# Centring, spread and norm products moved inside the two row scans

## The reference, cut to what matters

```python
def _L2_conv_ref(x, W):                 # layer 4's is the same with its own W
    rows = jnp.moveaxis(x, 1, 0)
    def step(carry, row):
        new = row + jax.nn.relu(conv1d_same(carry, W))     # 9 taps along the row
        return (new, new)
    _, outs = jax.lax.scan(step, rows[0], rows[1:])
...
def _ln_t(v, eps=1e-05):                # over the channels
    m = jnp.mean(v, axis=-1, keepdims=True); s = jnp.var(v, axis=-1, keepdims=True)
    return (v - m) / jnp.sqrt(s + eps)
...
x = x + _L2_conv_ref(_ln_c(x), L2_conv_W)          # scan 0
t = t + _L2_ffn_ref(_ln_t(t), ...)                 # experts, begins with gate logits of the norm
x = x + _L3_conv_ref(_ln_c(x), L3_conv_W)          # scan 1
t = t + _L3_ffn_ref(_ln_t(t), ...)                 # RNN: Wx, its mean and variance over the batch, 256 steps
```

## Time and profile before

| | |
|---|---|
| median of 3 runs | 385.49 us (384.47 to 387.49) |
| profiled execution, its own time | 385.72 us |
| its span (first to last instruction) | 383.9 us |
| mean granted clock of TensorE | 0.983 |
| PE busy | 346.4 us (90%) |
| DVE busy | 229.1 us (60%) |
| ACT busy | 191.1 us (50%) |
| chain that ended last, by engine | PE 64%, DVE 15%, ACT 13% |
| of it, row matmuls of the two scans (line 1076) | 6% |

### The profile page before, as it was taken

The page is one execution under the profiler, slowest core; times in us unless marked ns, Lnnn a source line. Parts: engine busy times, 40 slices in busy tenths (PEclk is TensorE's granted clock), DMA queues, the critical chain, the costliest instruction groups (busy, mean ns, idle before and its releaser), DMA issues.

```text
span 383.9 us, 9504 instructions
## 1 busy us (share of the span) xinstructions
PE 346.4 (90%) x4064; PEld 231.1 (60%) x4064; DVE 229.1 (60%) x461; ACT 191.1 (50%) x419; POOL 31.9 (8%) x37
## 2 busy tenths in 40 slices
PE   7967999999998999998988999799998899999990
PEld 2434555655645799974655369247746654773790
DVE  2679967767766522137846773762437366245884
ACT  1959678979748500026672646360247315033560
POOL 0024722121220000000000000000000000000000
PEclk9999999999999999999999999899999899999996
DMA  8982000000330000002000000000000000000004
GB/s 238 155 161 87 2 2 3 2 3 3 87 81 0 3 3 2 5 22 36 2 2 2 0 3 0 3 0 2 2 0 2 0 3 0 2 2 1 2 0 112
DMA packets 7338, 9.91 MB, mean 26 GB/s; under 512 B 3694, under 2 KB 6398, under 8 KB 6910
## 3 DMA queue, kind: packets, MB, share of 16 engines
q1 hardware_dynamic: 5630, 8.23, 10.3%
q10 hardware_dynamic: 1664, 1.05, 1.0%
HBM read 6.65 MB, written 1.05 MB: 20 GB/s over the span
## 4 chain that ended last, share of the span: by engine, by line
PE 64%; DVE 15%; ACT 13%; issue 5%; DMA 2%; SPq 0%; DVEq 0%; ACTq 0%
PE bank L646 28%; PE bank L1076 6%; PE bank L274 6%; PE bank L268 5%; PE bank L1006 4%; PE bank L1017 4%; PE bank L846 2%; ACT lnv L373 2%; PE bank L870 2%; DMA sb_consts<-in_consts 2%; ACT rs L378 2%; ACT arena L1242 1%; ACT arena L1244 1%; DVE arena L1771 1%; PE bank L1133 1%
## 5 line engine op out<-in xcount | busy, mean ns | idle before, releaser
L367 ACT ACTIVATE sq<-bank 128x512 f32<-128x512 f32 x33 | 19.4, 591 | 66.1 <-PE bank L268 50.7
L646 PE MATMUL bank<-xn,sb_w_attn 128*128 128x512 f32 x64 | 34.6, 622 | 6.8 <-ACT attn_scratch L1211 4.3
L646 PE MATMUL bank<-sb_consts 128*128 128x512 f32 (+1 forms) x84 | 37.4, 554 | 0.0
L274 PE MATMUL bank<-sq,sb_consts 128*128 128x512 f32 x66 | 34.7, 611 | 0.6 <-ACT sq L367 0.3
L373 ACT ACTIVATE lnv<-bank 128x512 f32<-128x512 f32 x33 | 19.7, 597 | 30.2 <-PE bank L274 29.9
L646 PE MATMUL bank<-arena 64*32 64x256 f32 (+4 forms) x466 | 26.7, 382 | 3.6 <-ACT arena L1244 2.2
L1076 PEld LDWEIGHTS bank<-arena,sb_w_late 128*128 128x128 f32 x180 | 23.0, 190 | 10.8 <-DVE arena L1829 7.6
L1017 PE MATMUL bank<-arena,sb_w_late 128*128 128x128 f32 x144 | 27.9, 276 | 0.0
L1006 PE MATMUL bank<-arena,sb_consts 128*128 128x128 f32 x144 | 27.7, 276 | 0.1
L1076 PE MATMUL bank<-arena,sb_w_late 128*128 128x128 f32 (+1 forms) x180 | 26.4, 283 | 1.4 <-DVE arena L1813 0.2
L1384 ACT ACTIVATE arena<-bank 128x128 f32<-128x128 f32 x72 | 20.0, 278 | 13.9 <-PE bank L1017 13.7
(11 more groups left out here) (207 smaller groups left out, 622.3 us busy)
## 6 DMA issues: line engine op xcount, KB each, us to landing
arena<-in_w_spec SPq DMA_DIRECT2D x2, 720.0 KB
sb_w_late<-in_w_late SPq DMA_DIRECT2D x1, 1100.5 KB, 24.3
arena<-arena SPq DMA_DIRECT2D x4, 256.0 KB, 4.1
arena<-fourier SPq DMA_DIRECT2D x1, 768.0 KB, 22.0
sb_w_attn<-in_w_attn SPq DMA_DIRECT2D x1, 641.0 KB, 9.7
xR<-in_x SPq DMA_DIRECT2D x4, 128.0 KB, 3.9
xR<-in_x ACTq DMA_DIRECT2D x4, 128.0 KB, 4.1
arena<-in_w_spec SPq DMA_DIRECT2D x2, 256.0 KB
```

The costliest lines, as they stand in the source:

```text
L274: pe.matmul(bank[:, var_bank(i), :], mean32, sq[:, i % 2, :], start=True, stop=True)\
L367: act.activation(sq[:, i % 2, :], bank[:, centre_bank(i), :], ACT.Square).then_inc(S("ln_squared"), 1)
L646: return mm(ps, lhsT, rhs, start=True, stop=True)
```

## The change

Three things are moved, in both scans unless said otherwise.

1. PE: `centre_next(j)` goes from row 4j+7 to row 4j+6, one row behind the second half of `rows_back(j)`. `ln_spread(j)` goes from row 4j+10 to row 4j+7. Row 6 has no `keep_busy` any more; rows 10 and 14, which had spreads, now have centrings, and rows 7, 11 and 15, which had centrings, now have spreads. `ln_spread(2)` so stands behind row 15 instead of behind `rows_back(3)`.
2. PE, scan 1: the first `wx` stands where `ln_spread(2)` stood, ahead of `centre_next(3)`, and the second ahead of `ln_spread(3)`.
3. DVE: `normalise(0)` goes from row 12 to row 10, `normalise(1)` from behind the loop to row 14. In scan 1 the statistics of quarters 0 and 1, not of 0 alone, stand ahead of `normalise(3)`.

```diff
-                    elif j >= 0 and turn == 3:
+                    elif j >= 0 and turn == 2:
                         centre_next(j)
-                    elif j >= 1:
-                        ln_spread(pe, ln_at(k + 1) + j - 1)
+                    elif j >= 0:
+                        ln_spread(pe, ln_at(k + 1) + j)
                     else:
                         keep_busy(BUSY_ROW, 3, P)
                 pe.wait_ge(S("row_done"), H * (i + 1))
                 rows_back(CH - 1, range(NQ))
-                ln_spread(pe, ln_at(k + 1) + 2)
+                if i == 1:
+                    wx(1, k + 1, 0)
                 centre_next(3)
                 if i == 0:
                     keep_busy(BUSY_BACK, 4)
                 else:
-                    wx(1, k + 1, 0)
+                    wx(1, k + 1, 1)
                 ln_spread(pe, ln_at(k + 1) + 3)
-                if i == 1:
-                    wx(1, k + 1, 1)
-                else:
+                if i == 0:
                     keep_busy(BUSY_LOGITS, 4)
...
-                for j in range([2, 1][i], CH):
+                for j in range(2, CH):
                     statistics(i, j)
...
-                    if h == 12:
-                        normalise(0)
-                normalise(1)
+                    if h in (10, 14):
+                        normalise(h // 4 - 2)
                 add_back(3)
                 normalise(2)
                 if i == 1:
-                    statistics(1, 0)
+                    for j in range(2):
+                        statistics(1, j)
                 normalise(3)
```

## The result

The changed kernel took 388.2 us (median of 11 runs, 386.84 to 390.29) against 386.05 us for the kernel before in the same session (11 runs). One run of the kernel before, at 462.54 us, was disturbed and is left out of the ratio of the two, which is 1.0065, 95% interval [1.0037, 1.0092]. The changed kernel is slower by about 0.65%. The forecast was 388.6 us and a rise of 2.98 us or 0.77%.

The account below looks back on a forecast made before the run. TensorE's program order was taken to bound the rows, fillers' waits delaying each scan. Per scan 1.78 lost less 0.25 gained, twice, less 0.08, gave +2.98 us: 388.6 us, range over all cases 385.7 to 390.3.

Parts of the forecast that it names:

- The centring's wait for the add: Rows 6, 10 and 14: the moved centring loads only after the add ends, 0.21 to 0.22 us late each.
- The spread's wait for the square: Rows 7, 11 and 15: the moved spread waits for ACT's square, 0.30 us each, delaying the next row.
- The wide filler in row 6: Row 6: the 512-column centring replaces the cheap 128-column `keep_busy`, costing 0.24 us per scan.
- The loop's sum: Rows up to quarter 3's transposes: filler and waits together lose 1.78 us per scan.
- Norm products at nothing: Rows 10 and 14 on DVE: the moved norm products cost nothing, covered by over 1 us; upper bound 0.69 us each.
- The tail: Each scan's tail: ACT, free sooner, starts the last square earlier, gaining 0.25 us; bounds 0 and 1.07 us.
- the chain's 1.07 us for the spread: Rival, each scan's tail: removing quarter 2's spread gains 1.07 us, with a whole statistic of 0.70 us; 386.4 us, chance 0.10.
- The statistics: End of scan 1: with two statistics after the last product, the last waits for the last `wx`; gain 0.08 us.
- The sum: Whole kernel: 1.53 us per scan, twice, less 0.08, gives +2.98 us; 388.6 us, chance 0.63.
- The clock's fall in scan 0's tail: Rival: a new 0.88 us TensorE gap lowers the clock, losing at most 1.7 us, up to 390.4 us; chance 0.14.

Follow-up runs that it names:

- square first: The kernel before, with ACT squaring quarter 3 ahead of the Exp of quarter 2 in each scan's tail; 384.75 us against 385.21 us, ratio 0.9989.

## Why the prediction was right

- **The centring's wait for the add**, 0.21 to 0.22 us a row: shown. It loads 0.06 us behind the add's end; halving the add takes 0.65 us off the loop, and moving the centrings alone puts 0.64 on.
- **The spread's wait for the square**, forecast as 0.30 us a row: shown, and about 0.28 us long. The spread loads 1.81 us behind the centring, where PE's order alone took 1.53; these 1.81 us are ACT's delay plus the square, and a shorter square shortens them by as much. The wait is additive to the first.
- **The wide filler in row 6**, forecast as 0.24 us: the rows agree. In the kernel before, the three row slots from row 6 on take 4.24 us with one narrow and one wide filler (264.14 to 268.38) and those from row 10 on 4.47 with two wide ones (269.79 to 274.26), 0.23 more; in the changed kernel both take 4.97.
- **The loop's sum** was forecast as 1.78 us and is 1.73; the difference is mostly the spread's wait. Row 15's DVE operation comes 1.44 us later after the scan's start (about 1.5 was forecast).
- **Norm products at nothing**: shown by putting them back, a difference of 0.01 us. The cover was thinner than "over 1 us": the row's own operation stands in the same 1.75 us, and behind the norm product DVE idled 0.85 us before row 11's operation.
- **The tail**: 0.25 forecast, 0.26 measured, and by the cause that was named, ACT's order and not PE's; two runs separate them (the unchanged 1.89 us in the changed kernel, the full gain in "square first"). The prediction set the chain's 1.07 us for the spread aside because the add releases the last centring. That is so, but the chain does not run over the centring; in the kernel before it runs from the spread over quarter 2's Ln and Exp to the last square:

```profile
280.01 1.07 PE bank L274 x2
...
281.10 0.61 ACT lnv L373
...
281.73 0.02 ACT rs L378
...
281.99 0.02 ACTq L372
...
282.27 0.59 ACT sq L367
```

  The runner-up, the last centring, would have let the square start at 281.99, only 0.28 us before it did. So 0.28 us was all that could be gained on this path with the centring where it was, and the 1.07 us of the spread were not on offer.
- **The statistics**: 0.08 forecast from the earlier trace rows, 0.08 measured.
- **The sum**: 2.98 us forecast, 2.86 in the scans' traces, and 0.65% [0.37%, 0.92%], or 2.5 us [1.4, 3.6], in the timing. The prediction held that a difference under 1% could not be told from none; eleven runs of each kernel tell this one, while the single profiled execution, 4.57 us longer, would have misjudged it.
- **The clock's fall in scan 0's tail**: did not happen: the granted clock stayed at 1.00 from 257 to 287 us, with the new gap of PE in it (0.81 us idle ahead of the last centring's matmul). The sentence that activity releases the throttle (the Trainium skill, TensorE: Matmul & The Clock Gate, Part 1) is not contradicted; this gap was no case of it.

## What to carry to other kernels

In a loop where two engines pass a short job back and forth, side work on an in-order engine is free only if its inputs are ready when its place in the list comes up; moved one slot nearer to its producer, as here, it made the loop wait 0.2 to 0.3 us a row for the producer. Before moving work off the tail, follow the chain to the instruction that is really held and ask what would release that one next: here the runner-up stood 0.28 us behind, so that no more than this could be won, and it was to be had by exchanging two instructions of another engine, at no cost to the loop. Where the same order of instructions stands elsewhere in the trace, its distances are a good price list: layer 2's RNN gave 2.68 us for the statistics, and 2.68 were measured.

## What was not expected of the hardware

Executions of one program differ by whole falls of TensorE's clock: the same kernel fell to 1.2 GHz three times or twice before its last few microseconds, in different places, and its span was 388.5 or 385.8 us. That difference of 2.7 us is nearly the whole of the effect that was studied, while the distances inside the two scans repeat to 0.01 us.

A 128x256 add from PSUM took DVE 0.42 us where the 128x512 one took 0.69, and a 128x256 square took ACT 0.38 us where the 128x512 one took 0.60: halving the work saved 39% and 37%, so that the halved square took 0.38 us and not the 0.34 I had assumed.
